# Both score stages of a chunked delta-rule recurrence issued as one, on all four 64x64 quarters of TensorE

## The reference

```python
xm = x + (shifted(x) - x) * (low_rank(mix) + time_maa)        # four inputs: rg, wa, k, v
r, k, v = xrg @ Wr.T, xk @ Wk.T, xv @ Wv.T                    # and the gates w, a, ma, mk, g of low rank
def step(s, inp):                                             # 4096 steps, state s of 32x32 per head
    q_, w_, k_, v_, a_, b_ = inp
    sa = einsum('bhij,bhj->bhi', s, a_)
    s = s * w_ + sa[..., None] * b_[:, :, None, :] + v_[..., None] * k_[:, :, None, :]
    return s, einsum('bhij,bhj->bhi', s, q_)
y = (group_norm(y) * ln_w + ln_b + bonus(r, k, v)) * g @ Wo.T
x = x + y
x = x + (int8(layernorm(x)) @ int8(Wffn).T) * scales + bias
```

## Time and profile before

| | |
|---|---|
| median of 3 runs | 3148.51 us |
| the profiled execution | 3128.81 us, span of its instructions 3126.8 us |
| granted TensorE clock, mean | 0.968 of full speed |
| TensorE busy | 2899.6 us, 93% |
| TensorE weight loads busy | 2566.1 us, 82% |
| VectorE busy | 2496.5 us, 80% |
| ScalarE busy | 1997.2 us, 64% |
| GpSimd busy | 1456.9 us, 47% |
| DMA engines, mean over the span | 55 GB/s |

### The profile page before, as it was taken

How to read it: one execution, slowest core, us unless ns; L and a number is a source line. 1 busy time by engine, 2 the same in 40 slices (tenths; PEclk the granted TensorE clock), 3 DMA queues, 4 the chain that set the end, 5 groups by cost and what they waited for, 6 DMA issues and landing times.

```text
span 3126.8 us, 176469 instructions
## 1 busy us (share of the span) xinstructions
PE 2899.6 (93%) x80128; PEld 2566.1 (82%) x80128; DVE 2496.5 (80%) x4803; ACT 1997.2 (64%) x4486; POOL 1456.9 (47%) x1224
## 2 busy tenths in 40 slices
PE   5999999999999999999999999999999999999995
PEld 5888888888888888888888888888888888888873
DVE  4787887878887888877788788888788887888875
ACT  4666666656666666656666666666666666666663
POOL 5445444445444454444444444544444544544542
PEclk9999999999999999999999999999999999999997
DMA  4122222222222222222222222222222222222211
GB/s 132 41 63 52 47 64 50 47 50 56 56 51 47 64 51 47 64 50 47 50 48 64 51 47 64 51 47 64 51 47 55 60 47 51 56 55 52 63 41 39
DMA packets 92610, 170.74 MB, mean 55 GB/s; under 512 B 13908, under 2 KB 14932, under 8 KB 91864
## 3 DMA queue, kind: packets, MB, share of 16 engines
q1 hardware_dynamic: 91864, 159.45, 21.6%
HBM read 41.97 MB, written 16.78 MB: 19 GB/s over the span
## 4 chain that ended last, share of the span: by engine, by line
PE 86%; issue 5%; DVE 5%; POOL 3%; ACT 1%; DVEq 0%; POOLq 0%; ACTq 0%
PE bank L1228 33%; PE bank_a L1367 12%; PE bank L1429 8%; PE bank_b L1398 4%; PE bank_b L1419 4%; PE bank_b L1345 4%; PE bank_a L1345 4%; PE bank L1235 4%; PE bank_b L1408 3%; PE bank L1310 2%; PE bank L1445 2%; POOL xm_wa L417 1%; PE bank_a L1383 1%; PE bank L1281 1%; PE bank_a L1375 1%
## 5 line engine op out<-in xcount | busy, mean ns | idle before, releaser
L537 ACT ACTIVATE bank<-bank,maa 128x128 f32<-128x128 f32 x1024 | 276.9, 385 | 103.2 <-PE bank L1281 103.2
L1006 DVE STREAM_TRANSPOSE stacked<-bank_b 32x256 f32<-32x256 f32 x512 | 229.2, 448 | 107.7 <-PE bank_b L1419 100.6
L1228 PE MATMUL bank<-xm_rg,w_r 128*128 128x128 f32 x2048 | 280.8, 285 | 7.6 <-issue 6.9
L1228 PE MATMUL bank<-xm_v,w_v 128*128 128x128 f32 x2048 | 281.8, 281 | 2.3 <-issue 2.1
L1429 PE MATMUL bank<-w_o,yc 128*128 128x512 f32 x512 | 259.2, 610 | 12.1 <-DVE yc L826 11.6
L1367 PE MATMUL bank_a<-pw,w_ffn_int 32*32 32x64 f32 x16384 | 258.7, 215 | 3.8 <-DVE pw L826 2.0
L1228 PEld LDWEIGHTS bank<-xm_rg,w_r 128*128 128x128 f32 x2048 | 243.7, 191 | 22.6 <-issue 8.4
L421 POOL TENSOR_TENSOR rs<-rs,minus_half 128x1 f32<-128x1 f32 x64 | 86.6, 1354 | 375.2 <-DVE rs L842 375.2
L1228 PEld LDWEIGHTS bank<-xm_v,w_v 128*128 128x128 f32 x2048 | 253.0, 194 | 8.5 <-issue 2.7
L1367 PEld LDWEIGHTS bank_a<-pw,w_ffn_int 32*32 32x32 f32 x16384 | 236.4, 105 | 23.9 <-issue 13.3
L1228 PEld LDWEIGHTS bank<-xm_k,w_k 128*128 128x128 f32 x2048 | 240.4, 193 | 10.8 <-issue 1.9
(11 more groups left out here) (188 smaller groups left out, 8127.5 us busy)
## 6 DMA issues: line engine op xcount, KB each, us to landing
streamed<-aq_state SPq DMA_DIRECT2D x128, 384.0 KB, 5.2
streamed<-w_ffn_int SPq DMA_DIRECT2D x128, 384.0 KB, 5.3
xin<-in_x SPq DMA_DIRECT2D x128, 128.0 KB, 5.0
xres<-in_x SPq DMA_DIRECT2D x128, 128.0 KB, 2.8
out<-o_sb SPq DMA_DIRECT2D x128, 128.0 KB
w_ffn_int<-in_weight_q SPq DMA_DIRECT2D x1, 2048.0 KB, 10.5
w_k<-in_Wk SPq DMA_DIRECT2D x1, 1024.0 KB
w_r<-in_Wr SPq DMA_DIRECT2D x1, 1024.0 KB
```

Of the source, the lines that this page charges most:

```text
L537: return nc.scalar.activation(out_, in_, func, **kw)
L1006: ins = V.transpose(to[:, :, 1 - c, :], step_part(NEW)[quad(h)])
L1228: ins = mm(bank[:, o * n:(o + 1) * n], weights[:, k, o * P:(o + 1) * P], x[:, k].rearrange("p b t -> p (b t)"), start=(k == 0), stop=(k == ...
```

## The change

**The score stages.** `scores_b` and `scores_k` become one stage, `scores`. For each group it issues four 64x64 matmuls: the two removal products as before, rows and columns of the array both those of the head pair, into `bank_a`; and the two key products with the columns exchanged (`two_heads(1 - pair)`), into the other half of `bank_b`'s partitions. The four lie on the four 64x64 quarters of the array. The stage waits for both kinds of pairs, and, because it writes `bank_b`, for the copy of the outputs of the previous tile's chunk 0 (`a_y`).

**The key scores.** As they now lie with the head pairs exchanged, `move_keys` takes them back in its DMAs: four of them instead of two, two with the transposed keys (`km[:, 2]`) and two with the masked scores (`km[:, 0:2]`), and the counts of `keys_moved` go from 32 to 64 per tile. VectorE must have masked the key scores before chunk 1 of the tile before may use `bank_b` (the new wait on `v_km`).

**The order.** The one stage stands right after `keys(i)`, ahead of `gates` and of chunk 1. The lists of all four compute engines are written out anew.

```diff
             def move_keys(m):
-                sp.wait_ge(v_km, count(m, 1, 1))
                 sp.wait_ge(v_klT, count(m, 1, 1))
                 sp.wait_ge(p_rhs, count(m, NC, 0))
                 for pair in range(2):
-                    sp.dma_start(streamed[:P // 2, :, pair], km[two_heads(pair)]).then_inc(keys_moved, 16)
+                    sp.dma_start(streamed[:P // 2, 2, pair], km[two_heads(pair), 2]).then_inc(keys_moved, 16)
+                sp.wait_ge(v_km, count(m, 1, 1))
+                for pair in range(2):
+                    sp.dma_start(streamed[:P // 2, 0:2, pair], km[two_heads(1 - pair), 0:2]).then_inc(keys_moved, 16)
...
-            def scores(bank, keys_):
-                for n, g, q in head_pairs([(g, g) for g in range(G)]):
-                    ins = mm(bank[q, 64 * n:64 * n + 64], both(keys_[q, g]),
-                             aq[q, :, g], start=True, stop=True)
-                return ins
-
-            def scores_b(m):
+            def scores(m):
+
                 pe.wait_ge(v_q, count(m, 1, 1))
                 pe.wait_ge(a_b2, count(m, 1, 1))
+                pe.wait_ge(a_k2, count(m, 1, 1))
                 pe.wait_ge(v_t, count(m, 1, 0))
-                scores(bank_a, bt2).then_inc(p_sb, 1)
-
-            def scores_k(m):
-                pe.wait_ge(a_k2, count(m, 1, 1))
-                pe.wait_ge(a_y, count(m, NC, 0))
-                scores(bank_b, kt2).then_inc(p_sk, 1)
+                if m >= 1:
+                    pe.wait_ge(a_y, count(m - 1, NC, 1))
+                for g in range(G):
+                    c = slice(64 * g, 64 * g + 64)
+                    for pair in range(2):
+                        q = two_heads(pair)
+                        ins = mm(bank_a[q, c], both(bt2[q, g]), aq[q, :, g], start=True, stop=True)
+                    if g == G - 1:
+                        ins.then_inc(p_sb, 1)
+                    for pair in range(2):
+                        q = two_heads(pair)
+                        ins = mm(bank_b[two_heads(1 - pair), c], both(kt2[q, g]), aq[q, :, g], start=True, stop=True)
+                ins.then_inc(p_sk, 1)
...
                 if c == 1:
                     pe.wait_ge(a_y, count(m, NC, 1))
+                    pe.wait_ge(v_km, min(count(m + 1, 1, 1), NT))
```

More of the change, by code:

```diff
@@ L761, in tile_step @@
                     inverse_deviation(n)
-                if project:
-                    exponentials(i)
+                if solve:
+                    power(m, 1)
                 if mix:
                     normalised(j)
-                if project:
-                    log_squares(i)
-                if solve:
-                    power(m, 1)
                 if finish:
@@ L776, in tile_step @@
                     front_transposed(j)
+                if project:
+                    key_decay(i)
+                    log_squares(i)
+                if solve:
+                    power(m, 2)
+                if project:
+                    key_deviation(i)
                 if solve:
                     output_gate(m)
-                if project:
-                    key_decay(i)
-                if solve:
-                    power(m, 2)
+                    value_pairs(m)
                 if project:
@@ L1092, in tile_step @@
                 j, m, n = i + 1, i - 1, i - 2
+                if solve:
+                    values_turned(m)
+                if mix:
+                    norm_input(j)
+                if solve:
+                    scores_k(m)
+                    bonus_rows(m)
+                    scores_b(m)
                 if finish:
@@ L1095, in tile_step @@
                 if mix:
-                    norm_input(j)
+                    norm_moments(j)
                 if solve:
-                    values_turned(m)
+                    keys_turned(m)
+                    scores_turned(m)
+                if project:
+                    decay_sums(i)
+                    removal_keys(i)
+                if solve:
+                    removals_turned(m)
                     values_summed(m)
-                    values_centred(m)
-                    scores_b(m)
-                    scores_turned(m)
                 if finish:
@@ L1155, in tile_step @@
                     residual_stats(n)
-                if solve:
-                    half_inverse(m)
-                if finish:
                     residual_moments(n)
                 if solve:
-                    half_turned(m)
+                    right_hand_sides(m, 0)
                 if finish:
@@ L1452, in tile_step @@
                     keys(i, [2, 3])
+                if solve:
+                    scores(m)
+                if project:
+                    gates(i)
                 if finish:
@@ L1455, in tile_step @@
                 if project:
-                    gates(i)
+                    decay_gate(i)
                 if finish:
                     solve_step(n, 1)
-                if solve:
-                    scores_b(m)
+                if project:
+                    queries(i, [0])
+                    queries(i, [1])
                 if finish:
@@ L1463, in tile_step @@
                 if project:
-                    queries(i, [0])
-                    queries(i, [1])
-                    decay_gate(i)
+                    queries(i, [2])
                 if solve:
@@ L1494, in tile_step @@
                     project_out(n, [1])
-                if mix:
-                    low_rank(j)
+                if solve:
+                    half_inverse(m)
                 if finish:
@@ L1499, in tile_step @@
                     project_out(n, [3])
+                if mix:
+                    low_rank(j)
                 if solve:
-                    half_inverse(m)
+                    from_values_and_state(m, 0)
                 if mix:
@@ L1504, in tile_step @@
                 if solve:
-                    from_values_and_state(m, 0)
                     inverse(m)
+                    solve_step(m, 0)
                 if mix:
```

141 lines of the change are left out of this document (59 added, 82 removed).

## The result

| | before | after |
|---|---|---|
| median of 4 runs each, side by side | 3143.45 us | 3189.13 us |
| ratio, 95% interval | | 1.0151 [1.0112, 1.0190] |
| profiled execution | 3128.81 us, span 3126.8 | 3195.75 us, span 3194.0 |
| granted TensorE clock, mean | 0.968 | 0.949 |

A forecast was written before the change was run, and what follows sets the result against it. TensorE's list, about 47 us for each of 64 tiles, plus its waits was taken as the bound. Terms -129 + 38 - 20 = -111 us took the 3148.5 us median to 3037 us, range 2980 to 3106.

The forecast's parts named there:

- 38: TensorE's waits for other engines: 1.2 us per tile in place of 0.6, so 38 us back; bounds -38 to +115.
- Instructions in time: "issue" waits for instruction packets, mostly in inverse: 20 us less, bounds -47 to +47.
- the order cost 103 us in place of 18: New order's forecast cost, 18 us: 38 of added waits less 20 of instruction waits.
- The score stage, -129: Joint score matmuls: four quarters run side by side, 128 records in 2.0 us, taking 129 us off TensorE's list.
- The wait for the key mask, 0.2 per tile: from_values_and_state of chunk 1, behind gates, waits some 0.2 us per tile for VectorE's mask of the key scores.
- `tx` and `xm_wa`, 0.8 per tile: Around the solve of chunk 0 and hidden layer, TensorE waits 0.8 us per tile; before, 0.6 on average.
- VectorE's run as the bound: Rival: VectorE's gap-free work from scores to next scores adds slips to the tile; 3139 us at 1.6 us slip, chance 0.08.
- The rival of this name: Instructions do not keep up: scores and inverse with the solve each cost L1383's wait again; 3104 us, chance 0.15.
- I am wrong if 'issue' grows beyond 150 us: Sign set for the next profile: "issue" waits above 150 us over the span would refute the forecast.
- DMAs and SyncE: Nothing: Four key-score transfers with the same bytes in place of two, landing in time; SyncE's issues have slack: no cost.

The follow-up runs named there:

- 1: Changed kernel with the key products on the same two quarters as the removal products, transfers without the exchange: 3238.66 us, 1.0331 of the kernel before.
- 12: Changed kernel with key products on the two removal quarters and key transfers issued only after the second power stage: 3211.84 us, 1.0267 of before.
- 2: Changed kernel with powers, half_inverse and inverse at two groups per matmul, half the instructions there, half of the products left out: 2951.73 us, 0.9409 of before.
- 3: Kernel before with powers, half_inverse and inverse at two groups per matmul, half the instructions there, half of the products left out: 2988.34 us, 0.9520 of before.
- 6: Changed kernel with the score stage alone at 128 instructions in place of 256, half of its products left out: 3103.56 us, 0.9912 of before.
- 9: Changed kernel with the four key transfers issued only after the second power stage, nothing left out: 3122.98 us, 0.9983 of before.
- 5: Changed kernel with the four key transfers per tile cut to a sixteenth of their bytes, same places and counts: 3106.39 us, 0.9932 of before.
- 11: Kernel before with its two key transfers per tile cut to a sixteenth of their bytes: 3136.89 us against 3129.15, 1.0024.
- 15: Changed kernel with late key transfers and powers, half_inverse and inverse at twice the columns per matmul, other results: 2952.94 us, 0.9388 of before.
- 4: Changed kernel with the solve of chunk 0 taking a constant in place of tx, so it does not wait: 3182.51 us, 1.0134 of before.
- 13: Changed kernel, scores between halves of keys, late key transfers, from_values_and_state before gates, solve before decay gate, nothing left out: 3133.24 us, 0.9963 of before.

## Why the prediction was wrong

The sum was -129 + 38 - 20. The step that failed is its last term, "Instructions in time", together with the "Nothing" for the DMAs and the granted clock, which had no term. By 1, the order cost 103 us in place of 18, and by the same run the quarters were worth 57 us in place of 129.

- **The score stage, -129: right as a length.** It takes 2.02 us for 128 records, and 3.88 without the exchanged quarters (1). By the Trainium skill ("TensorE: Matmul & The Clock Gate", on what overlaps), read as in the prediction, it would have stayed near 4 us; the measurement decides against that reading. As a gain in time it was wrong: what the quarters free was used for 57 of 119 us (1), and for 89 with the transfers late (12).
- **The wait for the key mask, 0.2 per tile: right in size.** The mask starts 0.1 us after the scores end and takes 1.23; the wait behind `gates` is 0.32 us in 47 tiles, 16 us in all.
- **`tx` and `xm_wa`, 0.8 per tile: right in size.** It is 67.6 / 64 = 1.06 us. With the mask the waits for other engines rose by 46 us, where 38 was forecast. The reason is not VectorE's run, though: the 1.10 us before the solve is `inverse`'s end, one addition of 0.41 us and the signals, and comes in every tile. VectorE's run as the bound did not happen; its busy share fell to 78%.
- **"Instructions in time", -20, bounds -47 to +47: the step that failed.** The stops within stages rose by 57 us and "issue" as a whole by 77. I had looked for places that use packets fast one by one, and moved the old wait about. But the quarters shorten the list and not the number of instructions: it is still ten packets per tile, in a list 2 us shorter. That the supply is the matter is shown by 2, 3 and 6: with fewer instructions the sign turns. That it is the packets' closest spacing is not: their starts are never under 3.2 us apart in either trace, but those on which a stop of over 0.3 us hung came 5.3 us (median) behind the one before in after, and 4.9 in before. The rival of this name had the mechanism, with +47 for the term; its 3104 is still 85 us short of the 3189 measured. "I am wrong if 'issue' grows beyond 150 us": it is 206.
- **"DMAs and SyncE: Nothing": failed.** I asked whether the transfers are in time, and not what they hold up. Their place costs 53 to 66 us (9), their bytes there 69 to 83 (5); in the old place nothing that shows (11), and with fewer packets next to nothing (15). This is part of the "issue" and the clock, not beside them.
- **Granted clock: not in my sum.** The 125 us more at the lower level are worth at most 62 us. I took stage lengths from a tile at 1.00 for a mean of 0.968. Taking away one kind of stop of TensorE did not lift the clock (4, still 328 us at the lower level), while fewer instructions, fewer bytes and later transfers did (5, 6, 9: 253 to 266 us). In 12 the time at the lower level is 266 us against 203 before, though the stops within stages are as long as before, so it does not go with late packets alone.
- **Where the 129 us went.** The balance above: 89 in slower work, 77 in "issue", 30 before the solve, sum 196, in the profiled executions. Late transfers (9) bring the change level with before, and even so the order costs 83 us (12), as much as the quarters then give.

Open: how the loss is split between late packets and the clock that follows them; why the new order costs 83 us with no more stops within stages than before, of which 39 are longer work; what sets the harmful place of the transfers apart from the harmless one; what decides that a packet is late; why 13 came out 13 us under before and not the 40 expected; what the new order would cost with the two score stages apart, which was not tried.

## What to carry to other kernels

Where TensorE is the bound and its matmuls are small, count instructions per microsecond beside columns: packing more tiles of the array saves time and no instructions, and where instruction packets already come late ("issue" within a stage whose inputs are there) part of the saving is paid back. Here, forms with half the instructions in five stages, which leave half of their products out, were 5 to 6% faster than before; a form that computes everything with fewer instructions was not tried. Tell such stops from "issue" waits of one length at the start of a stage, which are waits for data. Ask of each transfer that a change shifts not only when it is wanted but what else is under way where it lands. And price a new order by itself: a run with the new order and the old matmuls (1) showed it at 103 us.

## What the runs showed of the hardware

- Four 64x64 quarters run side by side: 16 ns a record in after against 30 for two (1), with all four writing two PSUM tensors, `bank_a` and `bank_b`.
- Packets of the instruction queue start at least 3.2 us apart (median 4.4 before, 4.6 after). With DMA traffic at 155 GB/s in one stretch a kernel with 632 of them was 53 to 66 us slower than with the key transfers later (9); with 472 of them the two were not told apart (15). By the Trainium skill ("Runtime: NRT & Kernel Launch", "Instruction fetch mechanics") fetches are hidden; here 119 and 176 us of stops within stages, before and after, show that they are not always.
- A stop of 1.1 us before the solve left the clock at 1.00 in a tile of before. In one of after it stood at 0.74 to 0.75 over the 6.7 us behind such a stop.
